# GAT layer of a graph network on one core: weighed rows split into a float32r rounding and its remainder, two float32r products per tile

## What is computed

```python
h = (x @ W).reshape(N, H, C)
a_src = jnp.sum(h * att_src, axis=-1)
a_dst = jnp.sum(h * att_dst, axis=-1)
logits = a_src[src] + a_dst[dst]
logits = jnp.where(logits > 0, logits, NEG_SLOPE * logits)
seg_max = jax.ops.segment_max(logits, dst, num_segments=N)
e = jnp.exp(logits - seg_max[dst])
denom = jax.ops.segment_sum(e, dst, num_segments=N)
alpha = e / (denom[dst] + EPS)
msgs = h[src] * alpha[:, :, None]
out = jax.ops.segment_sum(msgs, dst, num_segments=N)
```

## Time and profile before

| | |
|---|---|
| time, median of 3 runs | 6288.9 us (6285.21 to 6297.36) |
| profiled execution: span | 6290.0 us |
| layer 3 (3850 to 6290) | 2440 us |
| in it, PE busy | 1098.51 us |
| in it, DVE busy | 813.16 us |
| in it, ACT busy | 321.21 us |
| in it, POOL busy | 1526.48 us, 1612 gathers |
| in it, granted TensorE clock | 0.65 |

### The profile page before, as it was taken

How to read it: one execution, slowest core, us unless ns; L and a number is a source line. 1 busy time by engine, 2 the same in 40 slices (tenths; PEclk the granted TensorE clock), 3 DMA queues, 4 the chain that set the end, 5 groups by cost and what they waited for, 6 DMA issues and landing times.

```text
span 6290.0 us, 72860 instructions
## 1 busy us (share of the span) xinstructions
PE 4549.5 (72%) x24017; PEld 3664.1 (58%) x24017; DVE 2674.4 (43%) x9938; ACT 1822.6 (29%) x3934; POOL 3113.1 (49%) x3324
## 2 busy tenths in 40 slices
PE   6999978888888898888989995344444444544445
PEld 5888855666666566666669994234444343434334
DVE  8999943333333333333335442233333333333334
ACT  5888842222222222222224552011111111111112
POOL 0000036666666666666640004666666666666663
PEclk9999989999999999999999997666666666666667
DMA  6777765555555555555647784122222222222221
GB/s 152 166 163 167 164 162 178 178 179 177 180 176 179 179 177 179 179 179 177 182 133 220 244 243 112 44 48 48 47 47 48 49 48 47 47 50 48 48 48 29
DMA packets 473053, 804.93 MB, mean 128 GB/s; under 512 B 73183, under 2 KB 301706, under 8 KB 462698
## 3 DMA queue, kind: packets, MB, share of 16 engines
q0 software_dynamic: 140192, 443.73, 28.3%
q1 hardware_dynamic: 318378, 346.76, 18.1%
q10 hardware_dynamic: 14112, 9.74, 0.5%
HBM read 663.72 MB, written 136.22 MB: 127 GB/s over the span
## 4 chain that ended last, share of the span: by engine, by line
PE 47%; another core or an unknown queue 25%; DVE 12%; issue 11%; DMA 2%; ACT 2%; POOL 1%; DVEq 0%; ACTq 0%
PE bank L1034 12%; PE bank L1021 10%; PE bank L1205 7%; PE bank L689 5%; PE bank L669 3%; PE bank L1523 2%; DVE ring L987 2%; DVE ring L1415 2%; DMA atab<-at 2%; PE bank L1487 1%; PE bank L590 1%; POOL ring L550 1%; DVE hs L638 1%; PE bank L970 1%
## 5 line engine op out<-in xcount | busy, mean ns | idle before, releaser
L550 POOL DMA_INDIRECT ring<-ptab,src x1612 | 1526.9, 947 | 854.7 <-issue 446.2
L550 POOL DMA_INDIRECT ring<-htab,src x1612 | 1526.5, 947 | 853.1 <-issue 448.3
L1034 PE MATMUL bank<-ring,oh 128*126 128x384 f32 x3224 | 1257.8, 506 | 30.8 <-issue 30.3
L987 DVE TENSOR_TENSOR ring<-bank,ring 128x512 f32<-128x512 f32 x806 | 543.0, 687 | 1613.4 <-remote 855.2
L1021 PE MATMUL bank<-w1e,ea 128*128 128x256 f32 x3224 | 892.4, 400 | 252.2 <-DVE ring L987 190.9
L1021 PEld LDWEIGHTS bank<-w1e,ea 128*128 128x128 f32 x3224 | 620.1, 199 | 541.1 <-issue 270.9
L1523 PE MATMUL bank<-ring,oh 128*126 128x132 f32 x3224 | 675.6, 357 | 337.0 <-DVE ring L1415 224.6
L1003 ACT ACTIVATE ring<-ring 128x1024 f32<-128x1024 f32 x403 | 425.6, 1056 | 1400.5 <-DVE ring L987 1112.6
L1523 PEld LDWEIGHTS bank<-ring,oh 128*126 128x126 f32 x3224 | 583.5, 252 | 424.0 <-issue 219.9
L1034 PEld LDWEIGHTS bank<-ring,oh 128*126 128x126 f32 x3224 | 624.7, 196 | 290.5 <-issue 74.8
L689 PE MATMUL bank<-xhl,at 128*126 128x258 f32 x3822 | 712.6, 323 | 0.0
(11 more groups left out here) (268 smaller groups left out, 4727.0 us busy)
## 6 DMA issues: line engine op xcount, KB each, us to landing
atab<-at POOLq DMA_DIRECT2D x78, 1543.5 KB, 9.9
ring<-ea_r SPq DMA_DIRECT2D x403, 256.0 KB
ea<-ea_t SPq DMA_DIRECT2D x403, 256.0 KB
adjb<-atab SPq DMA_DIRECT2D x156, 535.5 KB, 4.6
adjb<-atab SPq DMA_DIRECT2D x78, 472.5 KB, 4.5
ring<-ptab,src POOLq DMA_INDIRECT x1612
ring<-htab,src POOLq DMA_INDIRECT x1612
ptab<-pO ACTq DMA_DIRECT2D x49, 128.0 KB, 7.3
```

The costliest lines, as they stand in the source:

```text
L550: return e.indirect_dma_start(o, None, table, bass.IndirectOffsetOnAxis(ap=src[:, t:t + 1], axis=0))
L987: e.tensor_tensor(group1(gi, m % 2), MLP[m % 3][:, :].rearrange("p (g f) -> p g f", g=2), group1(gi, m % 2), ALU.add).then_inc(s_edge, 1)
L1034: w = e.matmul(SUM[s % 2][0:SL, 0:384], slots_of(s, i), rv1[:, t // G % NR1, t % G, :], start=i == 0, stop=t == END[s])
```

## The change

In layer 3 the sum takes other inputs. The weighed rows of a chunk (weights too, 3 × 132 elements) are rounded to float32r by ACT into the first half of a buffer `split3` of NH3 = 7 chunks, and DVE subtracts that rounding from the rows and writes the remainder as float32r into the second half. PE then makes two float32r products per tile, of the rounding and of the remainder, into the same sum, in place of one fp32 product. New semaphores: s_high (rounding done) and s_rest (remainder done). POOL may reuse the ring's rows once the remainder of a chunk is done, in chunks of 3. ACT waits for s_sum3 of the chunk seven before, as the buffer wraps; s_sum3 now counts chunks.

Places move: weighing is done every 2 places (0, 2, ... 12) instead of every 3, rounding at the odd places, remainders at the even ones, and the sum of tile i at place i + LAG3 = i + 4, so that a group's sum ends in places 0 to 3 of the next step. ACT's copy of the sum goes from place 0 to 5, PE's add from 4 to 8, DVE's `slot_hots` from 0 to 17, where it waits for the end of the group before last; the tails open 5 places later. Outside of layer 3 only names and storage change: the one-hots `oh` are typed float32r and read through a fp32 view `ohf` in layer 1, the ring is declared once for each layer, and `at0` is set up later.

The core of the diff (left out: declarations of the ring, of `oh` and of `at0`, the fp32 view in the clearing of `oh`, and calls that pass `rows3` one argument more):

```diff
--- before.py
+++ after.py
@@ -115,7 +115,8 @@
     NBP = NB * P
     NR1 = 9
     NR3 = 4
-    RING = max(NR3 * GT * HROW, NR1 * G * 384)
+    CH = 3
+    NH3 = 7
     NEA = 5
     ND = 5
     NK = 4
@@ -518,6 +525,7 @@
             m3 = sb("m3", [P, 3, 4], c=l3)
             w3h = sb("w3h", [P, 3, 4], c=l3)
             part = sb("part", [P, 2, P], c=l3)
+            split3 = sb("split3", [P, NH3, CH, 2 * HROW], FR, c=l3)
             l3.close()
             gathering.close()
             halves2 = ExitStack()
@@ -558,9 +561,9 @@
                 e.bn_aggr(out=mv[:, :], in_=st[:, :]).then_inc(s, 1)
 
 
-            def slot_hots(e, s, s_oh, s_sum):
+            def slot_hots(e, s, s_oh, s_sum, summed):
                 if s >= 2:
-                    e.wait_ge(s_sum, END[s - 2] + 1)
+                    e.wait_ge(s_sum, summed)
                 e.tensor_tensor(slots_all(s), iota[:, 0:S].unsqueeze(1).broadcast_to([P, GT, S]),
                                 slot[:, START[s]:START[s] + GT].unsqueeze(2).broadcast_to([P, GT, S]),
                                 ALU.is_equal).then_inc(s_oh, 1)
@@ -1212,14 +1215,14 @@
                         tensor_post2(e, b, k)
 
 
-            W3 = weave(GT * (NS + 8), {GT * (s + 3) + 5: bs for s, bs in LASTS.items()}, 24)
+            LAG3 = CH + 1
+            W3 = weave(GT * (NS + 8), {GT * (s + 3) + LAG3 + 6: bs for s, bs in LASTS.items()}, 24)
             V3, A3 = 31, 3
             TOP3, LOG3 = 9, 3
-            CH = 3
-
             s_hots, s_pack, s_ohT, s_turn, s_rT, s_spread, s_o2, s_o2T, s_dst, s_top, s_most, s_logit_in, s_logit, s_exp, \
-                s_weigh = (sem(f"s_{n}") for n in ("hots", "pack", "ohT", "turn", "rT", "spread", "o2", "o2T", "dst", "top",
-                                                   "most", "logit_in", "logit", "exp", "weigh"))
+                s_weigh, s_high, s_rest = (sem(f"s_{n}") for n in (
+                    "hots", "pack", "ohT", "turn", "rT", "spread", "o2", "o2T", "dst", "top", "most", "logit_in", "logit", "exp",
+                    "weigh", "high", "rest"))
 
             CW = [sum(-(-n // CH) for n in SIZE[0:s]) for s in range(NS + 1)]
 
@@ -1227,9 +1230,14 @@
 
                 return START[s] % 2
 
-            def rows3(s, n):
-                o = s % NR3 * GT
+            def rows3(s, i, n):
+                o = s % NR3 * GT + i
                 return rv3[:, o:o + n, :]
+
+            def chunk(g, k):
+
+                n = CW[g] + k // CH
+                return n, split3[:, n % NH3, 0:min(CH, SIZE[g] - k), :]
 
             def weights3(o, n):
 
@@ -1239,8 +1247,8 @@
                 e.wait_ge(s_htab, 16 * NB)
                 for s in range(NS):
                     for i in range(SIZE[s]):
-                        if s >= NR3 and i % G == 0:
-                            e.wait_ge(s_sum3, START[s - NR3] + min(i + G, SIZE[s - NR3]))
+                        if s >= NR3 and i % CH == 0:
+                            e.wait_ge(s_rest, min(CW[s - NR3] + i // CH + 1, CW[s - NR3 + 1]))
                         gather(e, rv3[:, s % NR3 * GT + i, :], htab[:, :], START[s] + i).then_inc(landed3(s)[0], 16)
 
             def sync3(e):
@@ -1254,7 +1262,6 @@
 
                 n = TOP3 * s
                 if k == 0:
-                    slot_hots(e, s, s_oh3, s_sum3)
                     if s:
                         e.wait_ge(s_turn, 2 * s - 1)
                     e.tensor_tensor(hots[:, :, :], iota[:, 0:S].unsqueeze(1).broadcast_to([P, GT, S]),
@@ -1313,6 +1320,8 @@
                     z = bank[7][:, 16:16 + 8 * GT].rearrange("p (t q) -> p t q", q=8)
                     e.wait_ge(s_logit, LOG3 * s + 2)
                     e.tensor_tensor(zl[:, 0:m, :], zl[:, 0:m, :], z[:, 0:m, 4:8], ALU.subtract).then_inc(s_logit, 1)
+                elif k == 17:
+                    slot_hots(e, s, s_oh3, s_sum3, CW[s - 1] if s >= 2 else 0)
 
             def vector_post3(e, b, k):
                 n, z, d, x = V3 * b, small[:, 8:12], small[:, 16:20], hs[:, b, :]
@@ -1406,14 +1415,21 @@
                 e.wait_ge(s_hout2, NB)
                 e.wait_ge(s_clear2, 1)
                 for u in range(NS + 8):
-                    f, g = u - 1, u - 2
+                    f, g, c = u - 1, u - 2, u - 3
                     for k in range(GT):
-                        if 0 <= g < NS and k % CH == 0 and k < SIZE[g]:
-                            o, n = g % NR3 * GT + k, min(CH, SIZE[g] - k)
-                            m = rv3[:, o:o + n, 0:128].rearrange("p g (h c) -> p g h c", h=4)
+                        if 0 <= g < NS and k % 2 == 0 and CH * (k // 2) < SIZE[g]:
+                            i = CH * (k // 2)
+                            n = min(CH, SIZE[g] - i)
+                            m = rows3(g, i, n)[:, :, 0:128].rearrange("p g (h c) -> p g h c", h=4)
                             e.wait_ge(s_exp, 2 * g + 2)
-                            e.tensor_tensor(m, m, weights3(k, n).unsqueeze(3).broadcast_to([P, n, 4, 32]),
+                            e.tensor_tensor(m, m, weights3(i, n).unsqueeze(3).broadcast_to([P, n, 4, 32]),
                                             ALU.mult).then_inc(s_weigh, 1)
+                        if 0 <= g < NS and k and k % 2 == 0 and CH * (k // 2 - 1) < SIZE[g]:
+                            n, q = chunk(g, CH * (k // 2 - 1))
+                            w = rows3(g, CH * (k // 2 - 1), q.shape[1])
+                            e.wait_ge(s_high, n + 1)
+                            e.tensor_tensor(q[:, :, HROW:2 * HROW], w, q[:, :, 0:HROW].bitcast(F32), ALU.subtract).then_inc(
+                                s_rest, 1)
                         if 0 <= f < NS:
                             front3(e, f, k)
                         for b, j in W3[GT * u + k]:
@@ -1421,10 +1437,16 @@
 
             def scalar3(e):
                 for u in range(NS + 8):
-                    f, c = u - 1, u - 3
+                    f, g, c = u - 1, u - 2, u - 3
                     for k in range(GT):
-                        if 0 <= c < NS and k == 0:
-                            e.wait_ge(s_sum3, END[c] + 1)
+                        if 0 <= g < NS and k % 2 == 1 and CH * (k // 2) < SIZE[g]:
+                            n, q = chunk(g, CH * (k // 2))
+                            e.wait_ge(s_weigh, n + 1)
+                            if n >= NH3:
+                                e.wait_ge(s_sum3, n - NH3 + 1)
+                            e.activation(q[:, :, 0:HROW], rows3(g, CH * (k // 2), q.shape[1]), ACT.Copy).then_inc(s_high, 1)
+                        if 0 <= c < NS and k == LAG3 + 1:
+                            e.wait_ge(s_sum3, CW[c + 1])
                             if c >= 4:
                                 e.wait_ge(s_add3, c - 3)
                             for i in range(2):
@@ -1516,14 +1538,20 @@
                                 m = e.matmul(A[b % 2][:, 0:2 * X2W], oh2f[0:SL, c % 4, o:o + P], x2[0:SL, c % 4, :, :].rearrange(
                                     "p s q -> p (s q)"), start=c == SLO[b], stop=c == SHI[b])
                             m.then_inc(s_add3, 1)
-                        if 0 <= g < NS and k < SIZE[g]:
-                            e.wait_ge(s_weigh, CW[g] + k // CH + 1)
-                            if k == 0 and g >= 2:
-                                e.wait_ge(s_kept3, 2 * (g - 1))
-                            m = e.matmul(SUM[g % 2][0:SL, 0:HROW], slots_of(g, k), rv3[:, g % NR3 * GT + k, :], start=k == 0,
-                                         stop=k == SIZE[g] - 1)
-                            if k % G == G - 1 or k == SIZE[g] - 1:
-                                m.then_inc(s_sum3, k % G + 1)
+                        g, i = divmod(GT * (u - 2) + k - LAG3, GT)
+                        if 0 <= g < NS and i < SIZE[g]:
+                            n, q = chunk(g, i // CH * CH)
+                            if i % CH == 0:
+                                e.wait_ge(s_rest, n + 1)
+                            if i == 0:
+                                e.wait_ge(s_oh3, g + 1)
+                                if g >= 2:
+                                    e.wait_ge(s_kept3, 2 * (g - 1))
+                            for h in range(2):
+                                m = e.matmul(SUM[g % 2][0:SL, 0:HROW], slots_r(g, i), q[:, i % CH, h * HROW:(h + 1) * HROW],
+                                             start=i == 0 and h == 0, stop=i == SIZE[g] - 1 and h == 1)
+                            if i % CH == CH - 1 or i == SIZE[g] - 1:
+                                m.then_inc(s_sum3, 1)
 
             with nc.Block() as block:
                 block.gpsimd(lambda e: [f(e) for f in (pool0, pool1, pool2, pool3)])
```

33 lines of the change are left out of this document (17 added, 16 removed).

## The result

The changed kernel takes 6369.16 us (median of 4 runs, 6363.96 to 6380.11) against 6293.13 us (6285.21 to 6299.78) for the kernel before in the same comparison: a ratio of 1.0123, 95% interval 1.0107 to 1.0139. It is slower, by 76 us. The range held it; the likeliest case (6299) did not come. The time lies nearest to the rival on the other side (6387).

The account below looks back on a forecast made before the run. Layer 3 was taken as bound by the drain behind POOL's gathers, 1.40 of 1.469 us each. With ring, sum's end and other edits at 0 and the tail at +10, 6290.0 became 6300 by span, 6299 by median; range 6175 to 6400.

Parts of the forecast that it names:

- the likeliest case: Layer 3's gathers go on at 1.47 us and the tail gets 10: 6299 us by the median, chance 0.38.
- the rival on the other side: Layer 3: POOL's release waits behind weighing, rounding and subtraction, +88 us on 78 pauses; 6387 with the tail, chance 0.22.
- what holds the kernel before: Layer 3: PE's signals wait while POOL gathers, until the work behind drains at 1.40 of 1.469 us a gather.
- the one on the ring: Layer 3's ring: release by the remainder lets POOL gather longer but leaves the drain; 0, at best −107 us.
- The freed ring: Rival in layer 3: POOL restarts before the drain ends and the slack goes, 6192 us, half of it 6245; chance 0.34.
- DVE and ACT: Layer 3: subtractions of 0.56 us, 302 in all, fit DVE's waits; roundings of 0.57, 308 in all, cost 0 to 1.7 a step.
- PE: the term: Layer 3's sum: two float32r products save 240 to 340 us of PE, worth nothing by itself; a slower clock may cost +127.
- The sum's end: Layer 3: moving L564 and L1432 saves one of six hops a step, but the stall moves to ohT and away; 0.
- The tail: Steps after layer 3's last gather: new work shows, +10 us within +5 to +15, steps of 15 to 17 us.

Follow-up runs that it names:

- the second comparison: The changed kernel, unaltered, run again on a slow-draining chip against the kernel before: 6317.27 us against 6297.12, ratio 1.0037.
- `order_fp32`: Changed kernel's places with old arithmetic, POOL released by the sum; against the kernel before: 5532.06 us (0.9992) on the fast-draining chip, second run 6279.81 (0.9974) on a slow-draining one.
- `rest_psum`: Changed kernel with the remainder's second operand read from PSUM; against the kernel before: 5540.81 us (1.0008) on the fast-draining chip, 6461.22 (1.0259) on a slow-draining one.
- `high_only`: Changed kernel without the remainder, one float32r product per tile, POOL released by the rounding: 5540.15 us, 1.0007 of the kernel before, on the fast-draining chip.

## Why the prediction came out as it did

**Right: what holds the kernel before.** That PE's signals wait while POOL gathers, and that this sets POOL's stops on this chip, stood up to the tests: without gathers the waits vanish, a deeper ring gains nothing, and a spacing just above 1.40 us removes nearly all stops. That the drain takes just 1.40 us a gather is less sure, since signals are still 2.4 us late at a spacing of 1.43. And it holds for one kind of chip only, of which I didn't know: on another the gathers go at 1.25 us and no signal is late.

**Wrong: the likeliest case** ("gathers go on at 1.47 us"). The step that failed is the one on the ring: "From this edit: 0, at best −107 us". I reasoned that the drain sets the pace and that a release from DVE could only come sooner. A stop is the drain and then the way from the first released signal to POOL. Before, that way was short (1.3 us, in stops of 3.1). The remainder stands on DVE behind an instruction that waits for a held signal, and behind one more weighing (2.5 us, in stops of 5.1), and in 9 stops the way leads over one more round trip to PE. POOL stops less often and longer, 74 times in place of 109, and in sum 37 us more.

**Right in kind: the rival on the other side.** "Weighing, rounding on ACT and subtraction on DVE, where both engines stand in order behind waits for held signals (ACT's o2T, DVE's tops)" is what the timeline shows. Its price was 0.57 + 0.56 on each of 78 stops, +88. The way to POOL did get 1.2 us longer, near these 1.13, though of other parts: in the two stops shown above the rounding of the chunk is done before, and what stands ahead of its remainder is tops (0.69 us) and the weighing of the next chunk (0.54). The drain before it got 0.7 us longer; but the stops are 35 fewer, so that only 37 us of the 88 came, and 38 us are the gathers' own time, which no term had. These two errors nearly cancel, so that 6387 came close to 6369 by luck; the second comparison, at +20, is far from it. The rival's condition was met, yet it had 0.22 where the likeliest case had 0.38.

**The freed ring (0.34) did not come:** POOL's waits for the ring between 4200 and 6200 us, 203.4 + 132.6 = 336 us before, are 340 us for L1431 in the same window.

**DVE and ACT.** Sizes right: 0.564 us for 0.56, 0.531 for 0.57, which is below my line. What the remainder does to POOL's gathers through its second SBUF operand was missing.

**PE: the term was mis-sized in sign.** I gave a saving of 240 to 340 us; the sum's busy time rose from 675.6 to 743.4, and PE's in layer 3 to 1166.8, far above my 760 to 990. The step that failed is "two of 132 columns take about that, 0.14": I scaled the time of a float32r product of 256 columns with its columns. Twelve tiles back to back at full clock show that the time does not follow the columns. The first row is the fp32 sum of the second `order_fp32` run, the second the float32r sum of the changed kernel, the third the same at half the clock:

```profile
5635.65 2.87 PE L1538 MATMUL bank<-ring,oh 128*126 128x132 f32 x24
5618.19 2.87 PE L1551 MATMUL bank<-split,oh 128*126 128x132 f32 x24
5648.24 5.43 PE L1551 MATMUL bank<-split,oh 128*126 128x132 f32 x24
```

At full clock every record takes 0.12 us. One fp32 product has two of them and a float32r product one, so two float32r products of 132 columns cost the 0.24 us of the one fp32 product that they replace, and the product of 256 columns, at 0.13, hardly more than one of 132. So there was nothing to save. The rise is the clock's, which fell to 0.53, within my 0.5 to 0.65: 2534 of the sum's 3224 records ran wholly at half speed, 1104 before. How much of the 76 us it costs was not separated from the rest.

**The sum's end.** L564's wait (267.6 us) is gone from the list of waits and L1432's fell from 273.6 to 87.8, as forecast. The stall did not go to ohT and away, as I had said: ACT's waits for an unnamed signal before ohT fell from 292.2 to 239.0 us, and DVE's before tops rose from 341.9 to 440.2. The second `order_fp32` run, with all the moved places, gained 0.26%; the share of this edit in it was not measured.

**The tail: +10 forecast, +10.6 measured.** Two steps after the last gather:

```profile
6288.50:6303.29 14.79, 14.40 (x61) 13.60 (x62) 12.60 (x50) 5.56 (x16) 0.00 (x0) 0.50 0.01 2
6303.29:6318.90 15.61, 13.43 (x68) 12.21 (x68) 14.07 (x58) 8.82 (x20) 0.00 (x0) 0.66 0.01 4
```

The forecast was 15 to 17, and 14.79 falls just below; they were 13.30 and 12.70 before.

**What stays open.** Why the first comparison lost 76 us and the second 20, with the same kernel on chips where the one before takes the same time: the stops differ (74 of 5.1 us, 77 of 4.6), but what tips the rhythm was not found. Some of the difference is not of layer 3: in the second run layer 3 begins at 3831.7 us and not at 3849.2, which is 17 of the 40 us between the two profiled executions, and there is no trace of the kernel before on that chip to set beside it. POOL released by the sum on a slow-draining chip, and a paced version of the changed kernel, were not tried there. How much of the loss is the clock was not measured apart.

## What to carry to other kernels

When an engine stops to wait for a ring, ask not how early the new release comes on paper but what it stands behind in its engine's order: a release behind a late signal makes each stop longer, even where it makes the stops fewer. An added DVE operation with two SBUF inputs is not free because DVE has time; it can hold the gathers of POOL, and where POOL was the bound the holds were paid in full (30 us). On the other kind of chip, where POOL stops, a kernel without such holds was no faster (`rest_psum`). Before you count on a saving from another product type, compare the two back to back at one clock: here both forms cost 0.24 us a tile. If the signals of one engine come late only while another one gathers, try to space the gathers before rebuilding the chain, and run the same kernel on another chip before believing either.

## What the runs showed of the hardware

- The kernel before took 5536 us on one chip and 6293 to 6297 us in the other comparisons. By the traces of `order_fp32` there and of the kernel before here, a gather in layers 1 and 3 cost 1.25 us there and 1.47 us here, with the same busy time of 946 to 947 ns; the stops between are the difference.
- On the chips of the second kind PE's signals arrive late while POOL gathers: in the kernel before DVE's `tops` starts 4.7 us after PE's product on average (gathers 1.25 us apart), 6.8 at 1.31 us and 2.4 at 1.43 us. On the first chip it is 0.0 at 1.25 us.
- A DVE operation of 0.56 us with both inputs in SBUF that began up to 0.3 us before a gather makes the gather 0.25 us longer on average (up to 0.46); with one input in PSUM it does not (944 ns).
- Back to back at full clock, one fp32 product of 132 columns takes 0.24 us in two records, and two float32r products of 132 columns take 0.24 us too.
- With two float32r products per tile in place of one fp32 product the granted clock in 900 us without gathers was 0.63 and not 0.96, though PE was busy for 805 us and not 673. On the fast-draining chip, with the same places, it was 0.66 in layer 3 with the fp32 product (`order_fp32`), 0.55 with two float32r products (`rest_psum`) and 0.53 with one (`high_only`, PE busy 861 us against 896).
